# A decoder's weight splitter: VectorE's subtraction reads the high halves from PSUM, where TensorE copies them, for all but the last 512 columns

## The reference

```python
dt = softplus(ts @ dt_proj_w.T + dt_proj_b)
A = -exp(A_log)
def step(h, inp):
    dt_t, B_t, C_t, x_t = inp
    h = exp(dt_t[:, :, None] * A[None]) * h + (dt_t * x_t)[:, :, None] * B_t[:, None, :]
    return h, einsum('bdn,bn->bd', h, C_t)
y = scan(step) + x * D[None, None, :]
```

## Time and profile before

| | |
|---|---|
| Three timed runs | 3979.78, 3989.97, 3990.33 us, median 3989.97 |
| Profiled execution: its own time, its span | 3982.17 us, 3980.4 us |
| Busy share of the span: TensorE, VectorE, ScalarE, GpSimd | 88%, 80%, 40%, 35% |
| Granted TensorE clock, mean | 0.939 of full speed |

### The profile page before, as it was taken

One profiled execution on the slowest core, in us unless ns is written; L12 is line 12 of the kernel. 1 busy time (PEld: TensorE's weight loads), 2 busy tenths in 40 slices (PEclk: granted clock), 3 DMA queues, 4 the chain that ended last, 5 costly groups with the idle time before them and its releaser, 6 DMA issues. The chain is left out here.

```text
span 3980.4 us, 41707 instructions
## 1 busy us (share of the span) xinstructions
PE 3521.7 (88%) x15442; PEld 1475.8 (37%) x15442; DVE 3172.7 (80%) x2733; ACT 1609.0 (40%) x2189; POOL 1378.0 (35%) x493
## 2 busy tenths in 40 slices
PE   5777779989999979989999979989999988967999
PEld 1222243334333443334333443334433443324444
DVE  5999469887999869887999869887999869895333
ACT  5666343214655353214655353214655343213001
POOL 3454304362344304372344304372344304361000
PEclk9788899999899999989899999989899999978999
DMA  6678402121233302122233302122233302110222
GB/s 228 241 286 302 159 12 72 60 78 65 88 105 97 131 27 72 59 72 72 85 102 102 130 27 72 57 74 72 79 104 105 131 27 72 57 40 16 103 96 72
DMA packets 105431, 382.95 MB, mean 96 GB/s; under 512 B 14224, under 2 KB 27920, under 8 KB 102800
## 3 DMA queue, kind: packets, MB, share of 16 engines
q1 hardware_dynamic: 83632, 342.57, 24.6%
q10 hardware_dynamic: 21600, 37.73, 3.4%
HBM read 290.80 MB, written 64.32 MB: 89 GB/s over the span
## 5 line engine op out<-in xcount | busy, mean ns | idle before, releaser
L300 PE MATMUL ps<-r,ring 128*128 128x512 bf16 (+1 forms) x2040 | 781.4, 384 | 0.0
L297 PE MATMUL ps<-xr,ring 128*128 128x512 bf16 x1568 | 613.8, 391 | 1.4 <-PEq L2278 1.4
L301 PE MATMUL ps<-xr,ring 128*128 128x512 bf16 x1568 | 611.1, 390 | 0.0
L297 PE MATMUL ps<-r,ring 128*128 128x512 bf16 (+3 forms) x1384 | 545.4, 395 | 49.4 <-DVE xc L1102 17.8
L301 PE MATMUL ps<-r,ring 128*128 128x512 bf16 (+3 forms) x1384 | 544.8, 395 | 0.0
L1154 POOL TENSOR_TENSOR hh<-hh,bc 128x2048 f32<-128x2048 f32 x72 | 334.7, 4649 | 518.3 <-DVE hh L1064 518.3
L1154 POOL TENSOR_TENSOR bc<-bc 128x2048 f32<-128x2048 f32 x64 | 304.3, 4754 | 344.6 <-DVE bc L1064 344.6
L1154 POOL TENSOR_TENSOR r<-r,bc 128x2048 f32<-128x2048 f32 x56 | 260.9, 4658 | 297.7 <-DVE r L1064 297.7
L1064 DVE TENSOR_TENSOR_SCAN hh<-da,hh 128x2048 f32<-128x2048 f32 x72 | 325.7, 4523 | 1.3
L1105 DVE TENSOR_TENSOR xc<-xc,ps 128x512 f32<-128x512 f32 x176 | 119.5, 679 | 226.1 <-PE ps L301 225.8
L1064 DVE TENSOR_TENSOR_SCAN bc<-da,bc 128x2048 f32<-128x2048 f32 x64 | 296.0, 4625 | 0.5
(11 more groups left out here) (267 smaller groups left out, 6559.4 us busy)
## 6 DMA issues: line engine op xcount, KB each, us to landing
ring<-wsplit SPq DMA_DIRECT2D x216, 768.0 KB, 4.2
r<-wstream SPq DMA_DIRECT2D x54, 768.0 KB, 7.0
ring<-wsplit SPq DMA_DIRECT2D x76, 512.0 KB, 3.9
wsplit<-ring SPq DMA_DIRECT2D x38, 768.0 KB, 4.3
da<-r ACTq DMA_DIRECT2D x360, 63.9 KB, 2.1
wsplit<-r SPq DMA_DIRECT2D x14, 768.0 KB, 5.5
r<-wstream SPq DMA_DIRECT2D x19, 512.0 KB, 6.4
r<-xT SPq DMA_DIRECT2D x7, 1024.0 KB, 6.4
```

Of the source, the lines that this page charges most:

```text
L297: mm = pe.matmul(out, w_hi, x_hi, start=start, stop=False)
L300: pe.matmul(out, w_hi, x_lo, start=False, stop=False)
L301: return pe.matmul(out, w_lo, x_hi, start=False, stop=stop)
```

## The change

For the first scan alone, the splitter gets PSUM banks 6 and 7 as `show`. For each of VectorE's 21 slots TensorE multiplies the high half by the bf16 identity matrix into these banks, one matmul for every 512 columns and at most two. VectorE then subtracts the first 1024 columns with the high half read from PSUM, and what is left of the slot (512 columns of a slot of 1536, 64 of the one of 1088) as before, with both inputs in SBUF. A bf16 value is held exactly in a bank's fp32.

```diff
+    def show_high(self, pe, n, identb):
+        earlier = sum(self.by_dve(i) for i in range(n))
+        pe.wait_ge(self.high_done, n + 1)
+        if earlier:
+            pe.wait_ge(self.low_dve, earlier)
+        for c in range(2):
+            at = slice(c * T, min((c + 1) * T, self.columns[n]))
+            if at.stop > at.start:
+                mm = pe.matmul(self.show[:, c, 0:at.stop - at.start], identb, self.parts[n % SPLIT_RING][:, 0, at], start=True, stop=True)
+        mm.then_inc(self.shown, 1)
...
     def low_part(self, engine, n):
         engine.wait_ge(self.high_done, n + 1)
         at = slice(0, self.columns[n])
+        if self.show is not None:
+            from_bank = slice(0, min(2 * T, self.columns[n]))
+            at = slice(from_bank.stop, self.columns[n])
+            engine.wait_ge(self.shown, sum(self.by_dve(i) for i in range(n + 1)))
+            op = engine.tensor_tensor(self.parts[n % SPLIT_RING][:, 1, from_bank], self.whole[n % SPLIT_RING][:, from_bank],
+                                      self.show.rearrange("p c t -> p (c t)")[:, from_bank], ALU.subtract)
+            if at.stop == at.start:
+                op.then_inc(self.low_dve, 1)
+                return
         engine.tensor_tensor(self.parts[n % SPLIT_RING][:, 1, at], self.whole[n % SPLIT_RING][:, at], self.parts[n % SPLIT_RING][:, 0, at],
                              ALU.subtract).then_inc(self.low_pool if self.by_pool(n) else self.low_dve, 1)
...
                     if splitter.by_pe(n):
                         splitter.rest_part(pe, n, k.ident, k.minus)
+                    else:
+                        splitter.show_high(pe, n, k.identb)
...
-                            WeightSplitter(wstream, wsplit, spare(r1), ring_parts, others, 0, k.ps[:, 3:6, :]))
+                            WeightSplitter(wstream, wsplit, spare(r1), ring_parts, others, 0, k.ps[:, 3:6, :], k.ps[:, 6:8, :]))
```

More of the change, by code:

```diff
@@ L187, with __init__ @@
 class WeightSplitter:
-    SEMAPHORES = [f"landed{i}" for i in range(SPLIT_RING)] + [f"stored{i}" for i in range(SPLIT_RING)] + ["high", "low_dve", "low_pool", "low_act", "rest"]
-    def __init__(self, source, split, whole, parts, slots, pool_share, banks=None):
+    SEMAPHORES = [f"landed{i}" for i in range(SPLIT_RING)] + [f"stored{i}" for i in range(SPLIT_RING)] + ["high", "low_dve", "low_pool", "low_act", "rest", "shown"]
+    def __init__(self, source, split, whole, parts, slots, pool_share, banks=None, show=None):
+        self.show = show
         self.source, self.split, self.whole, self.parts, self.slots = source, split, whole, parts, slots
@@ L201, in begin @@
         self.landed, self.stored = sems[0:SPLIT_RING], sems[SPLIT_RING:2 * SPLIT_RING]
-        self.high_done, self.low_dve, self.low_pool, self.low_act, self.rest = sems[2 * SPLIT_RING:]
+        self.high_done, self.low_dve, self.low_pool, self.low_act, self.rest, self.shown = sems[2 * SPLIT_RING:]
     def by_pool(self, n):
@@ L217, in wait_low, with by_dve @@
             engine.wait_ge(self.low_dve, sum(not self.by_pe(i) and not self.by_pool(i) for i in range(n + 1)))
+    def by_dve(self, n):
+        return not self.by_pe(n) and not self.by_pool(n)
+    def show_high(self, pe, n, identb):
[8 more added lines that the diff above has]
+        mm.then_inc(self.shown, 1)
     def rest_part(self, pe, n, ident, minus):
```

## The result

| | before | changed |
|---|---|---|
| Timed runs, median | 3989.49 us (4 runs) | 4012.73 us (4 runs, 4003.97 to 4015.21) |
| Ratio to before, 95% interval | | 1.0061, 1.0042 to 1.0079 |
| Profiled execution: own time, span | 3982.17, 3980.4 us | 4003.97, 4002.2 us |
| First scan, end of scan step 0 to end of scan step 31 | 317.6 us | 336.9 us |

The change makes the kernel slower by 23 us by the medians. The forecast was 4003 us, +16.7, in a range from 3989 to 4015, slower by over 0.3% with a chance of 0.64. The two profiled executions differ by 21.8 us of span.

The account below looks back on a forecast made before the run. The prediction took VectorE as the bound, its two-SBUF-input instructions and GpSimd's excluding each other. Terms of +7.7, +5.6, +2.0, +1.5, +6.0, -2.7, -0.4 and -3.0 summed to +16.7 us, giving 4003 us, range 3989 to 4015.

Parts of the forecast that it names:

- The slot of 1536 columns, 11.86 us a round: Steps 0, 3, 15, 20, 27: the 512-column tail ends behind GpSimd, round 11.86 against 10.32 us, +7.7 us together.
- With line 1058 behind, 12.3: Steps 2, 14, 18, 26: line 1058 follows the tail, round 12.3 against 10.90 us, +5.6 us together.
- step 30, 11.4: Slot with a 64-column tail, which also waits for GpSimd: round 11.4 against 9.9 us, +1.5 us.
- slots without a tail, 8.9: Steps 8, 11, 12: 1024 columns from PSUM run under GpSimd's work, round 8.90 against 9.79 us, -2.7 us together.
- late high halves, -1.0 each: Steps 9, 23, 24: the first part runs under GpSimd, the tail ends 0.56 us behind it, -3.0 us together.
- Step 21, +2.0: `finish_y` loses its cover, which was GpSimd: round 12.3 against 10.32 us, +2.0 us.
- They are ready when the scan ends, since the high half is normally made one round ahead of it.: TensorE's copies come in time for VectorE; one up to 3 us late is hidden by GpSimd's 4.6 us.
- Steps 5, 17 and 29, +2.0 each: Steps where TensorE is late already: the tail delays its run of work, lengthening VectorE's wait, +6.0 us together.
- TensorE's copies, price 0: 41 copies, 17 us over 32 rounds, fit TensorE's free time: priced 0, bound +10 us.
- SyncE's later loads, price 0: Loads and stores go out up to 3.6 us later: priced 0, bound +3 us.
- The signs named: Profile after: GpSimd 4.5 us, line 291 3.9 to 4.2, line 286 1.2, step 5's TensorE wait near 6.5.
- rival 2: TensorE becomes the bound, late at about 10 places instead of 3: +27 us, or 4013 us; chance 0.12.

Follow-up runs that it names:

- the pair without GpSimd's work: Changed kernel and kernel before, each with GpSimd's first-scan product cut to 32 of 512 time columns: ratios to the kernel before 0.9980 and 0.9963.

## Why the prediction was right

The mechanism is shown, from four sides. The tail ends 0.54 us behind GpSimd in the changed kernel. Moved ahead of the other piece it takes 0.66 us. Cut off from a subtraction that never left SBUF it costs even more. And without GpSimd's work it takes 0.68 us.

- *The slot of 1536 columns, 11.86 us a round.* Right: 11.87 to 11.89 in four of five. Step 27 took 12.34, because its copy came 3.78 us late.
- *With line 1058 behind, 12.3; step 30, 11.4; slots without a tail, 8.9; late high halves, -1.0 each.* Right to 0.1 us: 12.27, 11.41, 8.90, -1.06.
- *Step 21, +2.0.* It was +2.7; the copy was 4.0 us late, behind a `rest_part`.
- *"They are ready when the scan ends, since the high half is normally made one round ahead of it."* This step failed, in its conclusion and not in its reason. TensorE waited for a high half ahead of a copy in only two places, 2.3 us. But the copy also waits for its place in TensorE's queue. Where VectorE's slot is the second of the pair it stands behind a `rest_part` (at step 21 the last of these matmuls starts at 334.52, and the copy at 334.74, while the high half was done at 329.72), and in the other steps behind the spreads. VectorE waited for copies in 16 of 21 places. That a copy up to 3 us late is hidden by GpSimd held, which kept the error small: outside steps 5, 17 and 29 the waits over 3.5 us, at steps 21 and 27, cost 0.7 and 0.5 us.
- *Steps 5, 17 and 29, +2.0 each.* Right in kind, and mis-sized: +1.0, +3.7 and +2.9. That the three add up to 7.6 where 6.0 were forecast is in part luck, since their errors have both signs. At step 17 the forecast put the tail inside the wait. It stands behind it, since its first piece needs the copy, which stands behind the late spread. At step 5 TensorE's run of work took 18.9 us (148.99 to 167.92) where the forecast gave it 19.8.
- *TensorE's copies, price 0.* Right in the kernel as it is: copies alone leave the time within 0.1%. It rests on GpSimd's cover, as the pair without GpSimd's work shows.
- *SyncE's later loads, price 0.* Right: loads made ScalarE wait 4.3 us in the changed kernel, 6.5 before. (The forecast's 3.8 us before was the first of two such rows; the other has 2.7.)
- *Nothing changes behind the scan.* The profile has 5.8 us there, at a lower granted clock; not forecast and not explained.
- *The signs named.* GpSimd's instruction takes 4.50 to 4.60 us at all 32 steps and line 286 never more than 1.22, as named. Line 291 takes 2.3 us on average over its 14 tails of 512 columns, where 3.9 to 4.2 were named, because a late copy makes the tail start later while its end stays 0.55 behind GpSimd. Where the copy is over 3.3 us late (steps 15, 17, 21 and 27) GpSimd is done by then, or within 0.1 us of it, and the tail takes 0.68. VectorE's wait at step 5 is 4.45 us for the copy, ahead of line 286, and not 6.5 for the spread. Line 286 does wait, idle and for TensorE, but never inside its own time, so this is not the sign against the mechanism that the forecast named.

The sum of the scan's rounds grew by 19.3 us where 16.7 were forecast, the block by 16.0, and the median of the runs by 23. That the median, 4012.7, meets the 4013 of rival 2 is chance: the rounds went as in the forecast, and what is above it lies partly behind the scan and is not explained.

## What to carry to other kernels

Where two engines exclude each other, an instruction's place in the order is its price: an instruction that stands straight behind the long one's release runs first and costs its length (0.66 us here), and 1 us later it costs what is left of the other's work as well (4.27 us). Moving most of an instruction off a contended side is worth nothing if what is left stands where the rest stood; put the part that must wait where its engine would wait anyway, and what doesn't need the side in between. Here that order and a share that spared the next bound, TensorE, turned a loss of 23 us into a gain of 19 over the kernel before.

## What the runs showed of the hardware

- Of two pieces of VectorE's, back to back and both with two SBUF inputs, the second did not keep the side: GpSimd, which had asked 1 us before, was served between them (5.00 us shown for 512 columns).
- The GPSIMD Engine Reference of the Trainium skill, section "Key points", names the contention for VectorE instructions with two SBUF inputs. The runs agree, and show its size: a whole instruction waits for the other's end, and 512 columns that take 0.68 us alone showed 5.00.
- TensorE's granted clock in unchanged code far behind the change differed, 0.86 for 0.90 in one stretch, while two profiles of the kernel before both took 3541.8 us behind the scan.
